# Cross-attention and routed FFN on one core: another order of the last stage, with GpSimd's sums and roundings behind VectorE's normalisations and routing

## What is computed

```python
x = x + xattn(layernorm(x), ctx)          # xattn returns its input plus attention
#   q, k, v = rmsnorm(h)*ln_w @ w_q.T, ctx @ w_k.T, ctx @ w_v.T
#   p = softmax(q k^T + position_bias, masked);  out = h + (p v) @ w_out.T
n = layernorm(x)
routing = softmax(n @ gate_w.T)                       # 8 experts
in_scale, out_scale = routing @ in_channel_scale, routing @ out_channel_scale
x = x + (n * in_scale) @ sign(weight).T * out_scale + bias
```

## Time and profile before

| | |
|---|---|
| median of 3 runs | 847.76 us (847.4 to 850.82) |
| profiled execution | 847.88 us, span 846.1 us |
| instructions | 12878 |
| VectorE, ScalarE, GpSimd busy | 625.4, 392.6, 301.4 us |
| mean DMA rate | 135 GB/s |

### The profile page before, as it was taken

How to read it: one execution, slowest core, us unless ns; L and a number is a source line. 1 busy time by engine, 2 the same in 40 slices (tenths; PEclk the granted TensorE clock), 3 DMA queues, 4 the chain that set the end, 5 groups by cost and what they waited for, 6 DMA issues and landing times.

```text
span 846.1 us, 12878 instructions
## 1 busy us (share of the span) xinstructions
PE 836.6 (99%) x4356; PEld 701.2 (83%) x4356; DVE 625.4 (74%) x1005; ACT 392.6 (46%) x1009; POOL 301.4 (36%) x279
## 2 busy tenths in 40 slices
PE   9999999999999999999999999999999999999998
PEld 8878888888888877888888888888888888888875
DVE  5777846778776786877777777777777777787775
ACT  5633422432431444544554554455555455547662
POOL 2103211022030053625444544544454454444144
PEclk9999999999999999999999999999999999999999
DMA  8354464673353759414224314412431431350002
GB/s 271 139 197 168 158 224 136 191 254 129 130 174 112 224 169 311 143 61 153 72 88 153 106 55 156 153 56 105 153 106 54 156 142 55 116 201 19 2 1 100
DMA packets 60720, 114.07 MB, mean 135 GB/s; under 512 B 5208, under 2 KB 38872, under 8 KB 55408
## 3 DMA queue, kind: packets, MB, share of 16 engines
q1 hardware_dynamic: 60656, 113.25, 39.0%
HBM read 77.58 MB, written 35.65 MB: 134 GB/s over the span
## 4 chain that ended last, share of the span: by engine, by line
PE 88%; DVE 7%; issue 2%; ACT 2%; DMA 1%; POOL 1%; DVEq 0%; POOLq 0%; ACTq 0%; SPq 0%
PE out L1325 10%; PE out L1327 10%; PE out L1326 10%; PE proj L1325 9%; PE proj L1327 9%; PE proj L1326 9%; PE o L1416 6%; PE s L1397 6%; PE s L1327 3%; PE s L1325 3%; PE s L1326 3%; PE t L1405 3%; PE proj L1492 1%; ACT probs L917 1%; PE proj L1493 1%
## 5 line engine op out<-in xcount | busy, mean ns | idle before, releaser
L917 ACT ACTIVATE probs<-probs,neg_max 128x128 f32<-128x128 f32 x256 | 99.7, 391 | 135.3 <-DVE neg_max L1170 135.2
L756 POOL TENSOR_TENSOR w_stage<-w_stage 128x256 f32<-128x256 f32 x30 | 25.1, 836 | 307.2 <-DMA w_stage<-in_wk 132.9
L768 POOL TENSOR_TENSOR w_lo<-w_stage,w_hi 128x512 fp32r<-128x512 f32 (+1 forms) x52 | 59.7, 1159 | 145.6 <-ACT w_hi L855 145.6
L1325 PE MATMUL out<-wo_hi,o_hi 128*128 128x512 f32 x224 | 95.2, 425 | 0.7 <-DVE acc L1202 0.6
L1202 DVE TENSOR_TENSOR acc<-out,acc 128x512 f32<-128x512 f32 x100 | 68.5, 688 | 33.7 <-PE out L1327 33.1
L1325 PE MATMUL proj<-x_hi,w_hi 128*128 128x512 f32 x210 | 88.5, 422 | 0.2 <-DVE ring L1029 0.2
L1327 PE MATMUL out<-wo_lo,o_hi 128*128 128x512 f32 x224 | 88.2, 394 | 0.0
L1326 PE MATMUL out<-wo_hi,o_lo 128*128 128x512 f32 x224 | 87.6, 391 | 0.0
L1327 PE MATMUL proj<-x_lo,w_hi 128*128 128x512 f32 x210 | 82.6, 393 | 0.0
L1326 PE MATMUL proj<-x_hi,w_lo 128*128 128x512 f32 x210 | 82.0, 390 | 0.0
L780 POOL TENSOR_TENSOR bias_mask<-bias_raw,mask_neg 128x512 f32<-128x512 f32 x64 | 75.2, 1186 | 11.0 <-DVE probs L1167 10.9
(11 more groups left out here) (352 smaller groups left out, 2152.1 us busy)
## 6 DMA issues: line engine op xcount, KB each, us to landing
k_spill<-ring SPq DMA_DIRECT2D x64, 256.0 KB, 2.8
v_spill<-ring SPq DMA_DIRECT2D x64, 256.0 KB, 2.2
w_stage<-in_wk SPq DMA_DIRECT2D x32, 256.0 KB, 3.3
big_stage<-in_wv SPq DMA_DIRECT2D x8, 1024.0 KB, 8.0
w_stage<-in_wq SPq DMA_DIRECT2D x32, 256.0 KB, 4.1
k_first<-k_spill SPq DMA_DIRECT2D x8, 1024.0 KB, 7.1
v_first<-v_spill SPq DMA_DIRECT2D x8, 1024.0 KB, 4.8
wo_raw<-in_wo SPq DMA_DIRECT2D x16, 512.0 KB, 3.3
```

The source lines that it names most:

```text
L768: pool.tensor_tensor(lo, staged(m, part), hi.bitcast(F32), ALU.subtract).then_inc(g_wlo, 1)
L917: last = act.activation(probs[:, j % 2, b, :], probs[:, j % 2, b, :], ACT.Exp, bias=neg_max[:, col:col + 1], accum_out=row_sum[:, col:col ...
L1325: pe.matmul(to[:], left_hi, right_hi, start=first and n == 0, stop=False, skip_group_check=True)
```

## The change

- `WO` becomes two steps, `WOH` (ScalarE) and `WOLO` (GpSimd). For all pairs but 15 they stand side by side, as before. For pair 15 `WOH` stays in unit 57, and `WOLO` moves to unit 59.
- The low parts of pairs 14 and 15 wait on GpSimd for the normalisations of units 56 and 59 (`v_probs`).
- `SCALES` (ScalarE) moves to the front of unit 56, and its low part, now `SCALESL` on GpSimd, behind `BM 58`.
- Scores 62 stand ahead of `OUT 15 1` and the statistics of tiles 0 and 1, instead of behind them.
- Of the last stage the order is another one. `T 63` stands ahead of the output product that it followed. On TensorE it is then, with names run together: T63 OUT14.6 TX0 PV63 TX1 GA0 OUT15.4 G0 TX3 TX2 OUT15.5 GA1 RT0 G1 OUT14.7 R0.0 R0.1 OS0 RT1 OUT15.7 R1.1 R1.0 TX4 OUT15.6 OS1 TX5 OS2 M0.0 GA2 M0.1 G2 M1.0 TX6 M2.0 TX7 RT2 M1.1 R2.1 R2.0 GA3 M2.1 G3 M3.0 OS3 M3.1 OS4 RT3 M4.0 R3.1 R3.0 OS5 M5.0 M4.1 M5.1 OS6 M6.0 OS7 M6.1 M7.1 M7.0. On GpSimd: BI1 BI0 BI3 BI2 BI4 YP0 BI5 YP1 SUM0 BI6 BI7 SUM1 YP2 SUM2 SUM3 YP3 SUM4 SUM5.
- On GpSimd `BI i` of tiles 2 to 7 waits for `ROUTE` number `i // 2 - 1` counted from 0, and `SUM i` of tiles 0 to 3 for `ROUTE 2` (tiles 0 and 1) or `ROUTE 3` (tiles 2 and 3).

```diff
@@ -81,7 +81,7 @@
-PARTS_OF = {"T": ("T", "PT"), "PV": ("PV", "OH", "OL"), "OUT": ("OUT", "ADD")}
+PARTS_OF = {"T": ("T", "PT"), "PV": ("PV", "OH", "OL"), "OUT": ("OUT", "ADD"), "WO": ("WOH", "WOLO")}
 def parts_of(step):
@@ -281,33 +281,34 @@
     j = 2 * SPLIT
     a, b, c = SPLIT // 2 - 1, SPLIT // 2, SPLIT // 2 + 1
     steps += [("FW",)]
-    steps += swift(j, outs(a, 3), outs(a, 4), [("WOL", c), ("SIGN", 0)])
-    steps += swift(j + 1, outs(a, 5), outs(a, 6), [("SIGN", 1), ("WO", c)])
-    steps += swift(j + 2, outs(a, 7), outs(b, 0), [("SIGN", 2), ("SCALES",)])
-    steps += swift(j + 3, outs(b, 1), outs(b, 2), [("SIGN", 3)])
-    steps += swift(j + 4, outs(b, 3), outs(c, 0), [*outs(c, 1), ("ST", 0)])
-    steps += swift(j + 5, [*outs(c, 2), ("ST", 1)], outs(c, 3), [])
+    steps += [("SCALES",)]
+    steps += swift(j, outs(a, 3), [("SCALESL",), *outs(a, 4)], [("WOL", c), ("SIGN", 0)])
+    steps += swift(j + 1, outs(a, 5), outs(a, 6), [("SIGN", 1), ("WOH", c)])
+    steps += swift(j + 2, outs(a, 7), outs(b, 0), [("SIGN", 2)])
+    steps += swift(j + 3, outs(b, 1), [("WOLO", c), *outs(b, 2)], [("SIGN", 3)])
+    steps += swift(j + 4, outs(b, 3), outs(c, 0), [])
+    steps += swift(j + 5, [*outs(c, 1), ("ST", 0), *outs(c, 2), ("ST", 1)], outs(c, 3), [])
     steps += slot(j + 6, [("ST", 2), ("ST", 3)], [("LN2", 0), ("ROOT", 0), *outs(b, 4)], outs(b, 5), [("LS", 0)], copy_first=True)
     steps = [part for step in steps for part in parts_of(step)]
-    steps += [("OUT", 14, 7), ("NT", 0), ("T", 63), ("NT", 1), ("TX", 0), ("PT", 63), ("BI", 1), ("TX", 1), ("TXC", 0), ("PV", 63), ("TXC", 1),
...
+    steps += [("T", 63), ("OUT", 14, 6), ("NT", 0), ("PT", 63), ("TX", 0), ("NT", 1), ("PV", 63), ("TXC", 0), ("BI", 1), ("TX", 1), ("OH", 63),
+              ("GA", 0), ("NT", 2), ("OL", 63), ("BI", 0), ("OUT", 15, 4), ("TXC", 1), ("NT", 3), ("G", 0), ("ADD", 15, 4), ("TX", 3), ("GM", 0),
+              ("ST", 4), ("GE", 0), ("TX", 2), ("OUT", 15, 5), ("ROUTE", 0), ("TXC", 2), ("TXC", 3), ("BI", 3), ("GA", 1), ("ADD", 15, 5), ("ST", 5),
+              ("RT", 0), ("BI", 2), ("G", 1), ("RTC", 0), ("OUT", 14, 7), ("GM", 1), ("LN2", 2), ("GE", 1), ("ROUTE", 1), ("R", 0, 0), ("R", 0, 1),
+              ("OS", 0), ("Y", 0, 0), ("RT", 1), ("ROOT", 2), ("OUT", 15, 7), ("RTC", 1), ("LS", 2), ("YH", 0, 0), ("Y", 0, 1), ("NT", 4), ("YL", 0),
+              ("R", 1, 1), ("R", 1, 0), ("OSC", 0), ("TX", 4), ("BI", 4), ("ADD", 15, 7), ("OUT", 15, 6), ("YH", 0, 1), ("ST", 7), ("NT", 5),
+              ("YP", 0), ("Y", 1, 0), ("OS", 1), ("TX", 5), ("ADD", 15, 6), ("OSC", 1), ("BI", 5), ("TXC", 4), ("OS", 2), ("ST", 6), ("M", 0, 0),
+              ("YH", 1, 0), ("LN2", 3), ("OSC", 2), ("GA", 2), ("Y", 1, 1), ("ROOT", 3), ("TXC", 5), ("M", 0, 1), ("LS", 3), ("YH", 1, 1), ("YL", 1),
+              ("G", 2), ("NT", 6), ("YP", 1), ("M", 1, 0), ("GM", 2), ("MP", 0), ("GE", 2), ("TX", 6), ("NT", 7), ("ROUTE", 2), ("M", 2, 0),
+              ("TXC", 6), ("SUM", 0), ("TX", 7), ("RT", 2), ("M", 1, 1), ("RTC", 2), ("TXC", 7), ("BI", 6), ("R", 2, 1), ("MP", 1), ("R", 2, 0),
+              ("GA", 3), ("Y", 2, 0), ("BI", 7), ("M", 2, 1), ("Y", 2, 1), ("YH", 2, 0), ("YL", 2), ("G", 3), ("SUM", 1), ("M", 3, 0), ("GM", 3),
+              ("MP", 2), ("GE", 3), ("OS", 3), ("YH", 2, 1), ("ROUTE", 3), ("M", 3, 1), ("OSC", 3), ("YP", 2), ("OS", 4), ("MP", 3), ("RT", 3),
+              ("M", 4, 0), ("RTC", 3), ("OSC", 4), ("SUM", 2), ("R", 3, 1), ("R", 3, 0), ("OS", 5), ("Y", 3, 0), ("M", 5, 0), ("SUM", 3),
+              ("Y", 3, 1), ("YH", 3, 0), ("M", 4, 1), ("YH", 3, 1), ("YL", 3), ("M", 5, 1), ("OSC", 5), ("YP", 3), ("MP", 4), ("OS", 6), ("MP", 5),
+              ("M", 6, 0), ("OSC", 6), ("SUM", 4), ("OS", 7), ("M", 6, 1), ("OSC", 7), ("SUM", 5), ("M", 7, 1), ("MP", 6), ("SUM", 6), ("M", 7, 0),
+              ("MPL", 1), ("SUML", 1), ("MPL", 0), ("SUML", 0)]
     return steps
@@ -492,7 +493,7 @@
                 return x_lo[:, 5], x_lo[:, 6]
             return wo_hi[:], wo_lo[:]
-        SCALES_AFTER = len([step for step in steps[:steps.index(("SCALES",))] if step[0] == "BM"])
+        SCALES_AFTER = len([step for step in steps[:steps.index(("SCALESL",))] if step[0] == "BM"])
         def output_bank(p, b):
             if p >= LAST - 1:
@@ -782,6 +783,9 @@
             def output_weights_low(p):
                 hi, lo = output_tiles(p)
+                if p >= SPLIT // 2:
+                    pool.wait_ge(v_probs, {SPLIT // 2: 2 * SPLIT, SPLIT // 2 + 1: 2 * SPLIT + 3}[p] + 1)
                 pool.wait_ge(a_wo_hi, p + 1)
                 pool.tensor_tensor(lo, wo_raw[:], hi.bitcast(F32), ALU.subtract).then_inc(g_wo_lo, 1)
@@ -794,6 +798,9 @@
                 if nth_bias["BI", i] == 1:
                     pool.wait_ge(d_ffn_small, 80)
                 pool.wait_ge(*normal_done(i))
+                if i >= 2:
+                    pool.wait_ge(v_routing, i // 2)
                 pool.tensor_tensor(acc[:, i, :], acc[:, i, :], ffn_bias_bc[:], ALU.add).then_inc(g_xb, 1)
             def scales_low():
@@ -814,11 +821,13 @@
                 if ("SUM", i) not in nth_pool_sum:
                     return
                 pool.wait_ge(v_prod, nth_scale_product["MP", i])
+                if i < HALF:
+                    pool.wait_ge(v_routing, i // 2 + 3)
                 pool.wait_ge(g_xb, nth_bias["BI", i])
                 pool.tensor_tensor(acc[:, i, :], acc[:, i, :], res_tiles[:, i % 2, :], ALU.add).then_inc(g_res, 1)
-            walk({"WS": pair_sums, "WX": query_weights_low, "BM": bias_and_mask, "WO": output_weights_low, "SMALL": clear,
-                  "SCALES": scales_low, "BI": ffn_bias_on, "YP": scaled_low, "SUM": last_sum})
+            walk({"WS": pair_sums, "WX": query_weights_low, "BM": bias_and_mask, "WOLO": output_weights_low, "SMALL": clear,
+                  "SCALESL": scales_low, "BI": ffn_bias_on, "YP": scaled_low, "SUM": last_sum})
         @block.scalar
         def _(act):
@@ -1002,7 +1011,7 @@
             walk({"DW": plain_weights_high, "DX": plain_ctx_high, "DC": plain_result, "E1": first_read, "C11": c11, "WX": weights_high, "VX": values_high, "CX": ctx_high, "LNR": layer_roots,
                   "RMSA": rms_roots, "X": x_transposed, "XX": x_high, "EXP": exponentials, "PT": transposed, "OH": out_high,
-                  "WO": output_weights_high, "SIGN": signs, "SCALES": scales_high, "ROOT": ffn_root, "NT": normal_tile, "TXC": ffn_transposed, "GE": router_exponentials,
+                  "WOH": output_weights_high, "SIGN": signs, "SCALES": scales_high, "ROOT": ffn_root, "NT": normal_tile, "TXC": ffn_transposed, "GE": router_exponentials,
                   "RTC": routing_transposed, "YH": scaled_high, "OSC": out_scale})
         @block.vector
```

More of the change, by code:

```diff
@@ L283, in schedule @@
     steps += [("FW",)]
-    steps += swift(j, outs(a, 3), outs(a, 4), [("WOL", c), ("SIGN", 0)])
-    steps += swift(j + 1, outs(a, 5), outs(a, 6), [("SIGN", 1), ("WO", c)])
-    steps += swift(j + 2, outs(a, 7), outs(b, 0), [("SIGN", 2), ("SCALES",)])
-    steps += swift(j + 3, outs(b, 1), outs(b, 2), [("SIGN", 3)])
-    steps += swift(j + 4, outs(b, 3), outs(c, 0), [*outs(c, 1), ("ST", 0)])
-    steps += swift(j + 5, [*outs(c, 2), ("ST", 1)], outs(c, 3), [])
+    steps += [("SCALES",)]
[5 more added lines that the diff above has]
+    steps += swift(j + 5, [*outs(c, 1), ("ST", 0), *outs(c, 2), ("ST", 1)], outs(c, 3), [])
     steps += slot(j + 6, [("ST", 2), ("ST", 3)], [("LN2", 0), ("ROOT", 0), *outs(b, 4)], outs(b, 5), [("LS", 0)], copy_first=True)
     steps = [part for step in steps for part in parts_of(step)]
-    steps += [("OUT", 14, 7), ("NT", 0), ("T", 63), ("NT", 1), ("TX", 0), ("PT", 63), ("BI", 1), ("TX", 1), ("TXC", 0), ("PV", 63), ("TXC", 1),
-              ("BI", 0), ("GA", 0), ("OH", 63), ("NT", 2), ("OL", 63), ("G", 0), ("OUT", 15, 5), ("GM", 0), ("GE", 0), ("TX", 2), ("NT", 3),
-              ("ADD", 15, 5), ("OUT", 15, 4), ("ROUTE", 0), ("TXC", 2), ("TX", 3), ("BI", 3), ("ADD", 15, 4), ("GA", 1), ("TXC", 3), ("ST", 5),
[12 rows of a table removed]
-              ("M", 7, 0), ("MPL", 1), ("SUML", 1), ("MPL", 0), ("SUML", 0)]
+    steps += [("T", 63), ("OUT", 14, 6), ("NT", 0), ("PT", 63), ("TX", 0), ("NT", 1), ("PV", 63), ("TXC", 0), ("BI", 1), ("TX", 1), ("OH", 63),
[14 rows of a table added]
+              ("MPL", 1), ("SUML", 1), ("MPL", 0), ("SUML", 0)]
     return steps
```

## The result

The changed kernel took 843.08 us in the median of 5 executions (842.7 to 844.16), the kernel before 847.76 us (847.24 to 850.82, 5 executions). The medians differ by 4.68 us (0.55%); the ratio worked out over all the executions is 0.9925, with a 95% interval from 0.9902 to 0.9949. So the changed kernel is faster, by 0.5 to 1%. Its median is 1.6 us better than the forecast of 844.7 and inside its range. I had given the most chance (0.62) to a change too small to tell; it can be told. The profiled execution took 844.16 us (span 842.4).

What follows compares the result with a forecast made beforehand. TensorE was taken as the bound, busy 836.6 of 846.1 us. Removed 5.65 and added 1.1 give -4.55 us without a clock fall, -3.1 with one, from 847.88 us: forecast 844.7 us, range 842.3 to 846.9.

Steps and rivals of the forecast that it cites:

- the low part of pair 14: W_O rounding on GpSimd waits for normalisation 56, so an output product's 0.6 us wait and its restart go: -1.11 us.
- normalisation 60: With pair 15's low part moved, this VectorE step runs undisturbed and transposition T60 doesn't wait: -0.85 us.
- RT0's wait: Transposition of the routing no longer waits, as bias additions 3 and 2 wait for ROUTE 0: -0.80 us.
- the waits at OUT15.4 and T63: New TensorE waits in the last stage: OUT15.4 for OL63, +0.4 us; T63 about 0.3 plus restart, net 0.
- Clock: Of two falls of TensorE's clock (1.36 and 1.53 us), the first goes; one stays around GA3, G3, at 1.45 us.
- the case without a fall: Rival: TensorE's clock doesn't fall at all, -4.55 us, giving 843.3 us; chance 0.28.
- The second fall's price: FFN half tiles at 826.86 to 830.37 took 3.51 us at half clock against 1.98: 1.53 us to gain.
- RT3 (+0.2): YP2 isn't gated and falls beside ROUTE 3: +0.2 us, bounds 0 and 1.1.
- OS2 (+0.4): OS1 and OS2 share a bank with one transposition between, so OS2 waits for a copy: +0.4 us, bounds 0.2 and 0.7.
- The new waits cost 0: GpSimd work queued behind the waits for the routing, and SyncE's stores, come later but stay covered: 0 us.
- The rival that GpSimd isn't the cause: GpSimd doesn't lengthen VectorE's small instructions; 1.11, 0.85 and 0.80 us stay lost, with two falls: 849.0 us; chance 0.05.
- The rival of four falls: Clock falls at all four places with router halves in the last stage, 1.45 us each: 849.1 us; chance 0.05.

Runs made afterwards that it cites:

- e6: Changed kernel without GpSimd's waits of the low parts of pairs 14 and 15 for normalisations 56 and 59; one execution, T56 to T62 31.26 us.
- e4: Kernel before with one edit: bias additions of tiles 2 to 7 wait for the routing of the pair before; median 847.32 us against 849.32, ratio 0.9983.
- a_again: Changed kernel, unedited, run once more; median 842.93 us of 6 executions, ratio 0.993 to the kernel before.
- e7: Changed kernel without the bias additions' waits for the routing, the last sums' waits kept; median 843.52 us against 842.93 for the changed kernel.
- e11: Changed kernel with OS2 behind M0.0, OS3 right behind R2.0, and YP2 waiting for ROUTE 3; median 843.69 us, ratio 0.9938 to the kernel before.
- e8: e4 with R3.0 moved up right behind R3.1; one execution, RT3 to the last matmul 11.95 us in place of 12.44.
- e9: Changed kernel with OS2 behind M0.0 instead of ahead of it; median 843.97 us of 6 executions.
- e3: Changed kernel without both GpSimd waits for the routing (bias additions and last sums), order kept; median 849.26 us, ratio 1.0011 to the kernel before.

## Why the prediction was right and wrong

Right, by its own steps: the low part of pair 14 (-1.11 forecast; -0.20 and -0.92 up to T57, and `e6` undoes the second with one wait); normalisation 60 (-0.85; T57 to T61 -0.87); the statistics (0; T61 to T62 3.99 and 3.95); RT0's wait (-0.80; `e4`, by one edit, 0.93 from T63 to RT0); the waits at OUT15.4 and T63. Normalisation 57 cost nothing (T56 to T57 5.00 us) where I had 0.1.

Wrong, and it makes the 1.6 us up to the median and 3.46 us by the profiled executions. The forecast's terms, put to the stretches of the table above:

| from ... to | forecast | measured |
|---|---|---|
| output 13.3 to T62 | -1.11 - 0.85 + 0.1 = -1.86 | -2.03 |
| T62 to RT0 | -0.80 + 0.4 = -0.40 | -0.76 |
| RT0 to RT1 | -1.36 | -1.55 |
| RT1 to the last matmul | -1.53 + 0.4 + 0.2 + 1.45 = +0.52 | -2.22 |
| sum | -3.10 | -6.56 |

So 2.74 of the 3.46 us lie behind RT1. From T62 to RT0 `e4` takes 14.82 us: RT0's wait gave 0.93, and the new order took back 0.17 where I had 0.4. The steps that failed:

- **Clock, the step that failed first.** "I expect a fall there, at the mean price 1.45." None in 10 of 11 executions (the 5 of the result and 6 of `a_again`). The place was right (`e7` falls there, at 1.49), its chance was not: it is a matter of the execution, and I had read one trace of before as if its two falls were a property of the kernel. I should have given the case without a fall, 843.3, the larger part.
- **The order's own price, a term that I didn't have.** I laid the new order out with fixed lengths and counted only waits. From RT1 to the last matmul, `e4` (old order, no fall) takes 31.57 us and the changed kernel 30.15: -1.42. Of that 0.70 is RT3's wait, which the old order lays open and the new one covers: the matmul ahead of RT3 is followed after 0.93 us in `e4`, where 0.23 is its usual distance. The other 0.72 are spacing. By kind of matmul the sums of start-to-start times are 14.74 (without that 0.70) and 14.58 us for the FFN products, 3.57 and 3.34 for the router, 2.20 and 1.90 for the input scales, 0.81 and 0.46 for the routing's transpositions, against +0.48 behind `TX` (OS2's wait among it). The old order passes 22 times between products of 64 and of 128 rows, the new one 18 times. At the 0.16 to 0.22 us of `e11` and `e8` four passages fewer are 0.6 to 0.9 us, less 0.21 for OS2's wait: an estimate of 0.4 to 0.7 for the 0.72.
- **The second fall's price, 1.53.** It was oversized as a gain: behind it stood RT3's wait, and `e4` shows 0.80 us from RT1 to the last matmul. The new order then covers that wait and gives 0.70, so the term came out at 1.50 by two errors that cancel. In the working on the fall, the "four half tiles" of 3.51 us are two half tiles, of four matmuls each; the price is not touched by it.
- **RT3 (+0.2) and half of OS2 (+0.4)** were too dear: 0 and 0.21 (0.19 idle; 0.21 saved by `e9`). The collision of YP2 with ROUTE 3 was there as forecast (1.40 us), and OS3 and OS4 ahead of RT3 covered it.
- **The routing's waits.** "The new waits cost 0" held, but I put their gain at ROUTE 0, by the bias additions. That is right for the old order (`e4`). In the new one `e3` shows ROUTE 0 clean without them and ROUTE 2 hit by SUM0, BI6 and BI7: the gain was two pairs later. It is large: 849.26 us without the waits against 842.9 to 843.5 with the sums' wait alone or with both, on another chip, each beside the kernel before; part of it is RT2's wait (RT1 to RT2 14.70 us in place of 12.54), part the falls, which came in half of the executions without them.

That the median lies 0.2 us from the no-fall case of 843.3 is luck: that case has 4.55 us for the change, the stretches show 6.56, and the medians of `a_again` and of before beside it are 6.37 apart. In the result they were 4.68 apart, as the 5 executions of before were 1.5 us shorter in the median (847.76) than the 31 and 12 of the later runs (849.32 and 849.3).

The prediction says of each long VectorE operation that it "ended just after" a GpSimd instruction. For the small ones that is 0.02 and 0.03 us. The 128x512 product of 777.24 ended 0.55 us after GpSimd's sum, near its own 0.69: it was held to the end of that instruction and ran then.

The rival that GpSimd isn't the cause is refuted by `e4`, where a wait of GpSimd's takes the long operations of ROUTE 0 away, and by `e6`, where taking a wait out brings those of normalisation 56 back. The rival of four falls didn't occur in any execution of the changed kernel.

## What to carry to other kernels

When VectorE's small operations on the critical path have lengths that make no sense for their size, look for the GpSimd instruction that ends with them, and put GpSimd behind them with a wait; one wait ahead of the first of a queue protects against all behind it, and taking work from between can lay open a collision that cost nothing before. A fall of the clock can hide such a wait too: take its price from a trace without the fall. An order has a price beside its waits: matmuls of 64 rows and of 128 rows should each stand in groups. And the clock's falls in one trace are one draw: take their number from many executions before they enter a sum.

## What the hardware showed that was not expected

- A fall of the clock can hold for 20 us with TensorE busy throughout (0.50 from 823.30 to 843.30 in `e3`), not only the 2.84 and 3.51 us of the earlier trace rows. Executions of the kernel before with a mean clock of 0.991 had spans of 850.0 to 851.5 us, those at 1.0 844.5 to 848.0.
- Between 64-row and 128-row products TensorE loses about 0.2 us at each passage, without an idle moment in the trace: two products of the input scales and two half tiles took 2.69 us in pairs and 3.12 one at a time, with two passages more.
